# Ten bfloat16 products of the identity ahead of each step's product, in the sum stage and the two maximum stages of a four-layer graph network

## The chip, the cores and the metric

The kernel runs on one core of one Trainium2 chip. The metric is the device time of one launch in microseconds (us), lower is better. Two runs of the kernel before gave 13,217.70 and 13,255.61 us, median 13,236.66 us.

## The reference, cut to what matters

Four graph layers over 6,250 nodes with 96 features and 206,250 directed edges sorted by destination, each followed by a residual and a layer norm. The change touches the edge work of the second layer (a segment sum) and of the two convolutions in the third (segment maxima):

```
# layer 1: sum over the edges of each node
msg  = relu(x[src] + edge_attr @ We + be)
aggr = segment_sum(msg, dst, num_segments=n)
h    = relu((x + aggr) @ W1 + b1) @ W2 + b2      # then batch norm, relu
...
# layer 2: twice, maximum over the edges of each node
msg  = x[src] @ W_msg + edge_attr @ W_edge
agg  = segment_max(msg, dst, num_segments=n)
c    = leaky_relu(where(isneginf(agg), 0, agg) + x @ W_root + b)
```

All of it is float32. Layer 0 is an attention over edges with a segment softmax, layer 3 a graph attention layer; neither is touched.

## The kernel before, in words

The program is a row of stages, each ended by a barrier: preparation, the edge stage of layer 0 (lines 685 and on, matmuls of lines 805, 812 and 829), a node stage, then `edge_pass("e1")` (sum), a node stage, `edge_pass("e2a")` (maximum), a node stage, `edge_pass("e2b")` (maximum), a node stage, the edge stage of layer 3 (line 1741 and on, matmuls of lines 1854, 1864 and 1868), and the last node stage.

`edge_pass` (line 1079) handles 1,024 edges in a step `s`, 202 steps a stage. Each engine runs its own queue in order and meets the others at semaphores:

- **POOL** issues eight indirect DMAs a step (line 1151), 128 rows of 96 floats each, from `x_tab` into `got[s % 3]`. Before the eight of step `s` it waits until the add of step `s - 3` is done (`v_add`).
- **SP** loads the edge attributes four steps ahead (line 1117, `load_attr(s + 4)`), the masks every second step (line 1122), and stores the results of step `s - 2` (line 1126), in this order. `load_attr(s + 4)` waits on `t_attr` at `s + 1`, the signal that the product of step `s` is finished.
- **PE** (TensorE) waits for the attributes of step `s` and for `v_add` at `s - 1`, so for the add of step `s - 2`, which read the same buffer `EA[s % 2]`. Every fourth step up to 49 times it first writes one node tile (a transpose at line 1166, or the product with the root weights at line 1164) into the free columns of `EA[s % 2]`. Then two float32 products of 128 x 128 by 128 x 384 (line 1168) go into the two banks of `EA[s % 2]`; the second adds one to `t_attr`. A float32 product stands in the trace as two MATMUL records, so a step has four, and a product with the root weights adds two.
- **DVE** (VectorE) waits in `add(s)` on `t_attr` at `s + 1` and on the landing of the eight gathers, empties the node tile where there is one (lines 1181, 1183, 1185), and adds `EA` and `got` (line 1187, `v_add`). It then transposes (line 1193), scans three times (line 1202) and transposes back (line 1210). In the sum stage ACT (ScalarE) applies the relu between add and transpose (line 1227).

In every stage of this kind two engines wait on the same value of `t_attr`: SP for `load_attr(s + 4)` and DVE for `add(s)`. A wait that the trace cannot match to a signal's source is shown as "remote".

Of the kernel before, what the change touches and what calls it, by code (L numbers as in the profile page):

```python
# [24 lines left out]
BF16 = mybir.dt.bfloat16  # L25
# [6 lines left out]
P = 128  # L32
# [69 lines left out]
def build(nc, t, n_nodes, n_edges, D, DE):  # L102
# [54 lines left out]
    with ExitStack() as top:  # L157
# [10 lines left out]
        def keepb(name, shape, dt=F32):  # L168
            return top.enter_context(nc.sbuf_tensor(name, shape, dt))

        X = keepb("X", [P, NT, D])
        R = keepb("R", [P, NT, D])
        ident = keepb("ident", [P, P])
        ones_f = keepb("ones_f", [1, P])
        eps_col = keepb("eps_col", [P, 1])
        part_col = keepb("part_col", [P, 1])
# [508 lines left out]
        with Phase("e0", group="edge") as ph, Phase("find0", group="node") as pf:  # L685
# [64 lines left out]
            def after(e, sem, count):  # L750
                if count > 0:
                    e.wait_ge(sem, count)
# [326 lines left out]
        def edge_pass(name, relu, mask_row, op0, op1, edge_w, root=None):  # L1079

            with Phase(name, group="edge") as ph:
# [9 lines left out]
                EA = [ph.ps(f"EA{i}", [P, 2, CH]) for i in range(2)]  # L1091
# [17 lines left out]
                def root_tile(s):  # L1109
                    return s // EVERY if s % EVERY == 0 and s // EVERY < NT else None  # L1110

                with nc.Block() as block:
                    @block.sync
                    def _(e):
                        def load_attr(s):
                            after(e, t_attr, s - RA + 1)
                            e.dma_start(attr[s % RA][:, :], t["attr_S"][s]).then_inc(s_attr[s % RA], 16)

                        def load_mask(b):
                            after(e, v_scan, 2 * (b - RM + 1))  # L1120
                            for i in range(4):
                                e.dma_start(mask[b % RM][32 * i:32 * i + 32, :], mask_c[i, b:b + 1].to_broadcast([32, MB * CHS])).then_inc(s_mask[b % RM], 16)

                        def store(s):
                            e.wait_ge(v_back, s + 1)
                            e.dma_start(out_c[s], out[s % 3][:, :, :].rearrange("p k d -> p (k d)")).then_inc(s_st[s % 3], 16)

                        load_attr(0)
                        load_mask(0)
                        for s in range(1, RA):  # L1130
                            load_attr(s)
                        load_mask(1)
                        for s in range(NS):
                            if s + RA < NS:
                                load_attr(s + RA)
                            if s % 2 == 0 and s // 2 + 2 < NB:
                                load_mask(s // 2 + 2)
                            if s >= 2:
                                store(s - 2)
                        store(NS - 2)  # L1140
                        store(NS - 1)
                        for i in range(3):
                            e.wait_ge(s_st[i], 16 * len(range(i, NS, 3)))
# [11 lines left out]
                    @block.tensor  # L1155
                    def _(e):
                        for s in range(NS):
                            e.wait_ge(s_attr[s % RA], 16 * (s // RA + 1))
                            after(e, v_add, s - 1)
                            q = root_tile(s)  # L1160
                            if q is not None:
                                after(e, root_done, q)
                                if root:
                                    e.matmul(EA[s % 2][:, 0, K * D:K * D + D], xT_all[:, q * P:(q + 1) * P], root_w[:, :], start=True, stop=True).then_inc(t_root, 1)
                                else:
                                    e.transpose(EA[s % 2][0:D, 0, K * D:K * D + P], X[:, q, :], ident[:, :]).then_inc(t_root, 1)
                            for h in range(2):
                                ins = e.matmul(EA[s % 2][:, h, 0:K * D], attr[s % RA][:, h * P:(h + 1) * P], edge_w[:, :], start=True, stop=True)  # L1168
                            ins.then_inc(t_attr, 1)
# [1060 lines left out]
```

## Time and profile before

| | |
|---|---|
| median of two runs | 13,236.66 us |
| span of the profiled execution | 13,179.5 us |
| busy PE, DVE, ACT, POOL | 4,527.1, 6,535.8, 1,994.5, 8,151.7 us |
| share of the span | 34%, 50%, 15%, 62% |
| mean granted TensorE clock | 0.541 of full speed |
| mean DMA throughput | 96 GB/s |

The span runs from the first to the last instruction of one profiled execution; the device time holds 57.2 us more than it. Busy time is what an engine spent inside instructions. The starts of PE's records are measured, their ends are modelled. "Idle before" is the gap ahead of an instruction on its engine, and the name behind the arrow is what ended it.

### The profile page before, as it was taken

What the parts mean: (1) busy time and instruction counts of PE and PEld (TensorE: products, weight loads), DVE (VectorE), ACT (ScalarE), POOL (GpSimd) and SP (SyncE); (2) the same over time, 40 slices, a digit from 0 to 9 for tenths busy, and PEclk for the clock granted to TensorE, in tenths of its full rate; (3) what the DMA queues carried; (4) which work ended last, traced back from release to release, by engine and by line L of the source; (5) the groups of instructions that cost most, each with busy time, mean ns of one, the idle gap of its engine ahead of it and who ended that gap; (6) DMA issues with size and microseconds to landing.
All of it is one profiled execution on the core that took longest, in us unless ns stands there. A gap on an engine that the chain in (4) does not pass through costs nothing. (4 is left out here: it accounts for less than half of the span.)

```text
span 13179.5 us, 81573 instructions
## 1 busy us (share of the span) xinstructions
PE 4527.1 (34%) x15877; PEld 3022.1 (23%) x15877; DVE 6535.8 (50%) x10237; ACT 1994.5 (15%) x4360; POOL 8151.7 (62%) x8551
## 2 busy tenths in 40 slices
PE   3354455555222222232222222222222234434443
PEld 3244344444110111111111111111111123333332
DVE  9543344444544454454445455444544544444445
ACT  3233333333100000010000000000000022222223
POOL 1455555555676666656666666766666666666665
PEclk7555555555555555555555555555555555555555
DMA  2355555555333333323333332333333222222222
GB/s 76 106 155 154 149 152 155 153 159 152 99 86 82 87 89 87 88 72 85 87 87 93 81 91 79 87 85 88 89 87 86 81 58 66 69 68 68 68 69 63
DMA packets 1007936, 1264.02 MB, mean 96 GB/s; under 512 B 483123, under 2 KB 740467, under 8 KB 1007331
## 3 DMA queue, kind: packets, MB, share of 16 engines
q0 software_dynamic: 303696, 520.91, 17.5%
q1 hardware_dynamic: 638139, 635.93, 14.8%
q10 hardware_dynamic: 65600, 101.96, 2.7%
q8 instruction: 136, 2.23, 0.1%
q14 instruction: 365, 2.99, 0.1%
HBM read 829.46 MB, written 428.44 MB: 95 GB/s over the span
## 5 line engine op out<-in xcount | busy, mean ns | idle before, releaser
L789 POOL DMA_INDIRECT e_got<-kv_tab,dst_cols x1661 | 1574.5, 948 | 1281.7 <-DVE e_pay L894 770.2
L1843 POOL DMA_INDIRECT e_got<-h_tab,src_tcols x1612 | 1540.9, 956 | 881.8 <-issue 473.8
L1151 POOL DMA_INDIRECT e2a_got<-x_tab,src_cols x1616 | 1531.3, 948 | 775.7 <-issue 556.2
L1151 POOL DMA_INDIRECT e_got<-x_tab,src_cols x1616 | 1553.5, 961 | 718.3 <-issue 586.9
L1151 POOL DMA_INDIRECT e2b_got<-x_tab,src_cols x1616 | 1531.3, 948 | 745.7 <-issue 518.8
L1168 PE MATMUL e2b_EA<-we_W_edge,e2b_attr 128*128 128x384 f32 x808 | 574.9, 866 | 1331.2 <-DVE e2b_emsg L1187 728.3
L1168 PE MATMUL e_EA<-we_We,e_attr 128*128 128x384 f32 x808 | 578.3, 871 | 1297.8 <-issue 898.1
L1168 PE MATMUL e2a_EA<-we_W_edge,e2a_attr 128*128 128x384 f32 x808 | 572.0, 862 | 1300.4 <-issue 767.3
L894 DVE TENSOR_TENSOR e_pay<-e_got,e_Q 128x384 f32<-128x384 f32 x416 | 230.2, 553 | 1570.4 <-ACT e_Q L962 1129.1
L1940 DVE TENSOR_TENSOR_SCAN e_run<-e_Z,e_run,e_msg 98x512 f32<-98x512 f32 x404 | 516.9, 1279 | 795.4 <-ACT e_msg L2005 619.8
L805 PE MATMUL e_Q<-e_window,e_pick 128*128 128x96 f32 x3328 | 758.9, 408 | 79.1 <-issue 41.2
L805 PEld LDWEIGHTS e_Q<-e_window,e_pick 128*128 128x128 f32 x3328 | 744.0, 327 | 84.8 <-issue 82.8
L812 PE MATMUL e_B<-ident,e_run 100*128 100x100 f32 x1664 | 374.5, 379 | 904.4 <-issue 493.3
L1854 PE MATMUL e_B<-ident,e_run 98*128 98x98 f32 x1616 | 357.1, 374 | 759.2 <-DVE e_run L1940 627.7
L1168 PEld LDWEIGHTS e2b_EA<-we_W_edge,e2b_attr 128*128 128x128 f32 x808 | 236.8, 323 | 1621.6 <-issue 1620.1
L829 PE MATMUL e_M<-ident,e_pay 128*100 128x128 f32 x1664 | 445.8, 422 | 470.0 <-DVE e_pay L894 366.4
L1168 PEld LDWEIGHTS e_EA<-we_We,e_attr 128*128 128x128 f32 x808 | 239.7, 327 | 1590.5 <-issue 1590.2
L1168 PEld LDWEIGHTS e2a_EA<-we_W_edge,e2a_attr 128*128 128x128 f32 x808 | 235.8, 321 | 1589.1 <-issue 1587.1
L845 DVE TENSOR_TENSOR_SCAN e_run<-e_keep,e_run,e_M 100x512 f32<-100x512 bf16 x416 | 532.3, 1280 | 11.5 <-issue 7.2
L1187 DVE TENSOR_TENSOR e2a_emsg<-e2a_EA,e2a_got 128x768 f32<-128x768 f32 x202 | 191.9, 950 | 692.4 <-remote 458.4
L1187 DVE TENSOR_TENSOR e2b_emsg<-e2b_EA,e2b_got 128x768 f32<-128x768 f32 x202 | 192.1, 951 | 671.5 <-remote 396.5
L1187 DVE TENSOR_TENSOR e_emsg<-e_EA,e_got 128x768 f32<-128x768 f32 x202 | 192.7, 954 | 648.3 <-remote 529.4
(373 smaller groups left out, 10316.0 us busy)
## 6 DMA issues: line engine op xcount, KB each, us to landing
scan_out<-e_out SPq DMA_DIRECT2D x416, 200.0 KB
e_window<-q_tab SPq DMA_DIRECT2D x1664, 48.0 KB
scan_out<-e_out SPq DMA_DIRECT2D x404, 196.0 KB
scan_out<-e_out SPq DMA_DIRECT2D x202, 384.0 KB
scan_out<-e2a_out SPq DMA_DIRECT2D x202, 384.0 KB
scan_out<-e2b_out SPq DMA_DIRECT2D x202, 384.0 KB
e_rel<-rel_row ACTq DMA_DIRECT2D x208, 256.0 KB
e_keep<-keep_row ACTq DMA_DIRECT2D x208, 200.0 KB
```

Source lines behind the costliest of these rows:

```text
L789: e.indirect_dma_start(got[i][:, k, :], None, kv_tab, bass.IndirectOffsetOnAxis(dst_c[:, c * K + k:c * K + k + 1], axis=0)).then_inc(s_g[i ...
L805: ins = e.matmul(Q[c % 3][:, k * D:(k + 1) * D], pick[c % 4][:, k, :], window[c % U][:, k, :], start=True, stop=True)
L812: ins = e.transpose(B[c % 2][:, k * PAY:(k + 1) * PAY], run[c % 3][:, k::K], ident[0:PAY, 0:PAY])
L829: ins = e.transpose(M[c % 3][0:PAY, k * P:(k + 1) * P], pay[c % 4][:, k, :], ident[:, :])
L845: e.tensor_tensor_scan(run[c % 3][:, :], keep[c // 2 % KR][:, at:at + CH], M[c % 3][0:PAY, :], run[(c + 2) % 3][:, CH - 1:CH], ALU.mult, A ...
L894: e.tensor_tensor(pay[c % 4][:, :, 0:D].rearrange("p k (h d) -> p k h d", h=HEADS), got[c % RG0][:, :, D:2 * D].rearrange("p k (h d) -> p ...
L1151: e.indirect_dma_start(got[s % RS][:, k, :], None, x_tab, bass.IndirectOffsetOnAxis(src_cols[:, q:q + 1], axis=0)).then_inc(edge_got[s % R ...
L1168: ins = e.matmul(EA[s % 2][:, h, 0:K * D], attr[s % RA][:, h * P:(h + 1) * P], edge_w[:, :], start=True, stop=True)
L1187: e.tensor_tensor(emsg[s % 3][:, :, :].rearrange("p (h k) d -> p h (k d)", h=2), EA[s % 2][:, :, 0:K * D], got[s % RS][:, :, :].rearrange( ...
L1843: e.indirect_dma_start(got[c % RG][:, k, :], None, h_tab, bass.IndirectOffsetOnAxis(src_tcols[:, q:q + 1], axis=0)).then_inc(s_g[c % RG], 16)
L1854: ins = e.transpose(B[v % 2][:, k * HW:(k + 1) * HW], run[v % 2][:, k::K], ident[0:HW, 0:HW])
L1940: V[v].give(e.tensor_tensor_scan(run[p][:, :], Z[p][0:HW, :], msg[p][:, :], run[q][:, CH - 1:CH], ALU.mult, ALU.add), "scan")
```

## The change

A helper `keep_busy` issues `n` matmuls whose weights and moving data are both views of the float32 identity read as bfloat16: 128 x 128 weights, 128 x 512 moving (two rounds over the 256 bfloat16 words of a row). In `edge_pass`, PE calls it with `n = 10` on the second bank of `EA[s % 2]`, behind the two waits of the step and ahead of the node tile and the product. The step's second product overwrites the bank's first 384 columns, and nothing reads the others there. The ten signal nothing. Each has its own weight load, so a step has 20 instructions of PE more.

```
+        ident_words = ident[:, :].bitcast(BF16)
+        def keep_busy(e, bank, n):
+            for i in range(n):
+                e.matmul(bank, ident_words[:, 0:P], ident_words.unsqueeze(1).to_broadcast([P, 2, 2 * P]), start=True, stop=True)
...
                         for s in range(NS):
                             e.wait_ge(s_attr[s % RA], 16 * (s // RA + 1))
                             after(e, v_add, s - 1)
+                            keep_busy(e, EA[s % 2][:, 1, :], 10)
                             q = root_tile(s)
```

## Rows read from the trace of the kernel before

**Rows 1.** The page, its first line.
```profile
span 13179.5 us, 81573 instructions
```

**Rows 2.** The view of line 1187 (the add): duration ns min/median/max, first and last start us.
```profile
L1187 DVE TENSOR_TENSOR e_emsg<-e_EA,e_got x202: 915/957/959, 3452.0 to 5711.5; 128x768 f32<-128x768 f32 x101
L1187 DVE TENSOR_TENSOR e2a_emsg<-e2a_EA,e2a_got x202: 910/956/959, 5854.8 to 8107.1; 128x768 f32<-128x768 f32 x101
L1187 DVE TENSOR_TENSOR e2b_emsg<-e2b_EA,e2b_got x202: 911/957/959, 8218.6 to 10476.5; 128x768 f32<-128x768 f32 x101
...
  remote: 1384.2, 284
```

**Rows 3.** Windows, gathers of line 1151 alone: POOL busy (count), PEclk, DMA share, GB/s.
```profile
3440.00:3640.00 200.00, 151.09 (x160) 0.54 0.35 96
...
5843.00:6003.00 160.00, 120.94 (x128) 0.55 0.35 95
6060.00:6260.00 200.00, 131.06 (x135) 0.53 0.30 80
```

**Rows 4.** Timeline, early in stage e2a: start us, us, engine, line, xcount [idle before].
```profile
5877.43 2.82 PE L1168 MATMUL e2a_EA<-we_W_edge,e2a_attr 128*128 128x384 f32 x4
...
5880.28 0.33 SPq L1117 DMA_DIRECT2D e2a_attr<-in_attr_S  x1
...
5884.55 0.96 DVE L1187 TENSOR_TENSOR e2a_emsg<-e2a_EA,e2a_got 128x768 f32<-128x768 f32 x1 [3.05 <-DMA e2a_got<-x_tab,src_cols]
```

**Rows 5.** Timeline, 300 us later in the same stage.
```profile
6154.10 0.35 SPq L1117 DMA_DIRECT2D e2a_attr<-in_attr_S  x1
6154.11 0.96 DVE L1187 TENSOR_TENSOR e2a_emsg<-e2a_EA,e2a_got 128x768 f32<-128x768 f32 x1 [5.59 <-remote]
...
6155.21 2.90 PE L1168 MATMUL e2a_EA<-we_W_edge,e2a_attr 128*128 128x384 f32 x4 [7.93 <-issue]
...
6164.07 0.94 POOL L1151 DMA_INDIRECT e2a_got<-x_tab,src_cols  x1 [0.30 <-issue]
6169.49 0.33 SPq L1117 DMA_DIRECT2D e2a_attr<-in_attr_S  x1
6169.50 0.32 DVE L1185 SCALAR_TENSOR_TENSOR R<-e2a_EA,rstd_all,r_l2b 128x96 f32<-128x96 f32 x1 [9.76 <-remote]
...
6170.83 2.90 PE L1168 MATMUL e2a_EA<-we_W_edge,e2a_attr 128*128 128x384 f32 x4 [12.72 <-DVE e2a_emsg L1187]
```

**Rows 6.** Timeline of SP, the next three loads of attributes.
```profile
6182.09 0.35 SPq L1117 DMA_DIRECT2D e2a_attr<-in_attr_S  x1
...
6193.29 0.33 SPq L1117 DMA_DIRECT2D e2a_attr<-in_attr_S  x1
...
6204.52 0.35 SPq L1117 DMA_DIRECT2D e2a_attr<-in_attr_S  x1
```

**Rows 7.** Windows: PE, PEld, DVE, ACT, POOL busy (count), PEclk, DMA share, GB/s.
```profile
6165.10:6169.40 4.30, 0.00 (x0) 0.00 (x0) 0.00 (x0) 0.00 (x0) 0.00 (x0) 0.50 0.05 11
5740.00:5840.00 100.00, 58.52 (x192) 38.35 (x192) 66.62 (x263) 42.87 (x79) 35.05 (x35) 0.74 0.16 39
...
2100.00:2900.00 800.00, 428.32 (x1926) 371.12 (x1925) 365.04 (x601) 252.05 (x600) 455.89 (x482) 0.52 0.56 156
11000.00:13000.00 2000.00, 825.38 (x4524) 640.69 (x4522) 950.83 (x2417) 521.12 (x1090) 1272.60 (x1338) 0.54 0.27 68
```

**Rows 8.** Timeline, a catching-up stretch of stage e2a, two adds in turn.
```profile
6373.40 0.91 DVE L1187 TENSOR_TENSOR e2a_emsg<-e2a_EA,e2a_got 128x768 f32<-128x768 f32 x1
...
6378.91 0.92 DVE L1187 TENSOR_TENSOR e2a_emsg<-e2a_EA,e2a_got 128x768 f32<-128x768 f32 x1
```

**Rows 9.** Groups of PE by form of line 1864: busy us, mean ns of one.
```profile
L1864 PE MATMUL e_Z<-e_parts,e_sel 80*98 80x128 bf16 x1616 | 252.2, 308 | 113.3 <-issue 74.0 <-DVE e_mid L1979 25.4 <-DVE e_parts L1981 10.5
```

**Rows 10.** Timeline, layer 3's edge stage.
```profile
12013.95 0.70 PE L1854 MATMUL e_B<-ident,e_run 98*128 98x98 f32 x4
...
12017.33 0.50 ACT L1999 ACTIVATE e_out<-e_B 128x392 f32<-128x392 f32 x1 [4.85 <-remote]
...
12061.43 0.63 PE L1864 MATMUL e_Z<-e_parts,e_sel 80*98 80x128 bf16 x4
```

## The prediction

> **What bounds the kernel now.** I read the view of the add first, since each of the three stages repeats one add per step. From first to last add a stage takes 2259.5, 2252.3 and 2257.9 us [rows 2], over 201 intervals: 11.24, 11.21 and 11.23 us a step. Then the gathers, the one engine with enough work to fill that: a gather takes 0.94 us and 0.30 us of gap [rows 5], so eight need at least 9.92 us. The windows say that POOL reaches its pace only at the start of a stage. It issues 160 gathers in the first 200 us of the sum stage and 128 in the first 160 us of e2a, 10.0 us a step both times. From 6060 to 6260 us it issues 135 in 200 us, 11.9 us a step [rows 3]. Something other than POOL costs 1.2 us a step on average.
>
> Two timelines name it. Early in e2a the product starts at 5877.43 and its records end at 5880.25. SP, which waits on `t_attr`, goes at 5880.28, and DVE's next add is released by a landing gather [rows 4]. So the product's signal comes on time there, and nobody on the path wants it. 300 us later SP and DVE start within 0.01 us of each other, at 6154.10 and 6154.11 and again at 6169.49 and 6169.50; DVE's waits are "remote" now [rows 5]. The one semaphore that `load_attr(s + 4)` and `add(s)` share is `t_attr`, at the same value. Just before the second of these pairs nothing runs: from 6165.10 to 6169.40 all five engines are at 0.00, and the DMA share is 0.05 [rows 7]. The last gather was issued at 6164.07 and POOL cannot go on, as its next gather waits for this add. So the add waits for the product's signal.
>
> The records of PE hide this. The only product recorded between the two adds, 6155.21 to 6158.11 [rows 5], is not even the one awaited at 6169.5: that one, by the double buffer, was issued after the add before 6154.11. **The signal comes some 20 us after the product's recorded start.** Four steps with one node tile take from 6154.10 to 6204.52 [rows 5, 6], 50.4 us for 16 records of products and two of the tile: 2.8 us a record, where on time four take 2.82 us together [rows 4]. Steps of 11.20 us between signals (6182.09 to 6193.29, [rows 6]) are four such records. TensorE's signals leave at a quarter of the rate at which it seems to work. DVE's waits of this kind sum to 1384.2 us in 284 cases [rows 2]; that is no saving yet, because DVE would wait for gathers instead.
>
> **When does it lag?** Not behind dense matmul work. A stretch of a node stage has 192 records in 100 us with a clock of 0.74 [rows 7], and the stages that follow start on time. In a late stretch a step has 4.5 records in 12.6 us. The edge stages of layers 0 and 3 give 1926 records in 800 us and 4524 in 2000 us, 0.42 and 0.44 us a record [rows 7]. They lag at times (line 1854 ends at 12014.65, its reader goes at 12017.33 on "remote", 2.7 us late [rows 10]), but cannot be at 2.8 us a record. I take it that sparse work on TensorE brings the lag, which is argued from these densities and not shown. The granted clock does not tell it: it is 0.53 to 0.55, mostly the 1.2 GHz level, in early and late windows alike [rows 3].
>
> The Trainium skill ("TensorE: Matmul & The Clock Gate", section "Seeing it yourself") warns that the recorded clock events are unreliable and that the clock has been seen stuck at K=1/4; by that a product of 2.82 us would take 11.3, and the trace agrees in size, with 11.20.
>
> **The change, part by part.** It adds ten matmuls a step, 606 steps, and removes nothing.
> *Their time on PE.* The nearest bfloat16 rows: four of 128 columns take 0.63 us [rows 10], one takes 0.308 [rows 9], so they start (0.63 - 0.31)/3 = 0.107 us apart, and 512 columns take 0.43. Ten are 4.3 us. Bound from above: four float32 records of 384 columns take 2.82 us [rows 4], 0.70 each, scaled to 512 columns 0.94, ten 9.4. Bound from below: half of 4.3, at the 2.4 GHz level. I take 4.3, the same type. A step of PE is then 4.3 + 2.9 = 7.2 us, with a node tile of two records (another 0.7) 7.9, under the 10.0 of POOL.
> *On the path?* The product starts behind the add of step `s - 2` and is needed by the add of step `s`, 20 us later. 20 less 7.9 leaves 12 us of cover, also for the 2.7 us of lag in rows 10. If the cover goes, a step costs what PE takes.
> *First step of a stage.* PE needs 4.3 + 0.7 + 2.9 = 7.9 us; eight gathers need 9.92 and a landing. Hidden.
> *SP.* `load_attr(s + 4)` waits 4.3 us longer, and the masks and the store of step `s - 2` stand behind it. The store was ready when DVE ended its chain of 5.5 us [rows 8]; it now goes up to 3 us later. Its buffer is needed three steps on, 30 us; the attributes are needed four steps on. Nothing.
> *DVE, ACT, POOL.* No instruction more; the ten write a bank whose reader is done. Nothing, while a step of DVE (5.5 us [rows 8]) stays under 10.0.
> *The gain.* If 7.2 us of work in 10 keeps TensorE out of the lag, the gathers pace every step as in the first 160 to 200 us: 201 x 10.0 = 2010 us a stage. Saved: 249.5 + 242.3 + 247.9 = 739.7 us. The span goes from 13,179.5 [rows 1] to 12,439.8; the device time holds 57.2 us more (the median, 13,236.7, less the span), so **12,497 us**, 5.6% less. Late next are the gathers. At 9.92 us a step it would be 48 us less; at 10.3, with relapses, 180 us more.
>
> **The rivals.** What about 2% separates from no change, some 265 us.
> *1. Half a cure (0.15).* The lag returns in a part of the steps, as in layer 3's edge stage, which has a record each 0.44 us and still lags. Against it: 12 us of cover. At half the gain, 12,870 us.
> *2. No effect (0.13).* The lag has a cause outside TensorE's load. For it: the last edge stage lags with a dense load. Against it: on-time starts of the stages. The ten fill idle time: 13,237 us.
> A page's rule gives the same. By the Trainium skill, same page, Part 1, activity lifts the clock from 1.2 to 2.4 GHz. That would halve a recorded product of 2.9 us which the records show hidden in 11.2, and so change nothing; the trace speaks against reading the records so, since the add does wait for the signal [rows 5].
> *3. Slower (0.17).* The lag stays and charges the ten as it charges the others. The place is the same wait of the add. A step has 14.5 records instead of 4.5, and gets slower than 11.22 us if a record takes over 0.77 us on average. At 2.8 us it adds 28 us to each late step, with 9 in 10 of 606 late 15,300 us: 28,500 us in all. Against it: 0.42 us a record in the dense stages. A milder form needs no lag: at the float32 rate a step of PE is 9.4 + 2.9 + 0.2 = 12.5 us, 603 x 1.28 = 770 us more, 14,010 us.
>
> **How the numbers follow.** The cure has 0.55, and a range of its own of 12,420 to 12,700 (9.92 and 10.3 us a step, with the spread of the runs). Faster by over 2%: 0.55 and 0.15, together 0.70. Within 2%: 0.13. Slower: 0.17. The range from 12,420 to 13,280 takes in the cure, the half and no effect, and leaves out the slower cases.
>
> **What would show it.** Right: 8 gathers in 10.0 us through all three stages; DVE's waits before line 1187 end by gathers, not "remote"; SP and DVE no longer start together; stage lengths near 2010 us. The granted clock may rise to the 2.4 GHz level, which is no part of the sum. Wrong: equal starts of SP and DVE stay, with steps of 11.2 us (rival 2) or near 40 (rival 3); or PE's records of the ten lie more than 0.8 us apart.

## The result, and the profile after

The change made the kernel slower by 1.3%: median 13,408.4 us (13,400.8 to 13,416.0) against 13,236.7 us, ratio 1.0131, 95% interval 1.0099 to 1.0163. That is clear of the spread of these runs, two of each kernel, and less than 2%. I had forecast 12,497 us and a range up to 13,280.

The kernel before took 13,110 to 13,240 us in three sessions of this study (a session is a row of kernels run on one chip) and 11,236 us in three others, so the times of whole runs are compared with the kernel before of the same session, and I call the two kinds **late** and **on time**, after what the signals of TensorE do there. The pair of the forecast is from a late session; beside the kernel before at its best, 11,236 us, the change is worth nothing either way (eight runs, ratio 0.9999, below).

The page of the changed kernel, its first line, and then the view of the add, line 1194 in this kernel (columns as in [rows 2]):

```profile
span 13414.1 us, 93693 instructions
```

```profile
L1194 DVE TENSOR_TENSOR e_emsg<-e_EA,e_got x202: 902/920/958, 3444.5 to 5763.8; 128x768 f32<-128x768 f32 x101
L1194 DVE TENSOR_TENSOR e2a_emsg<-e2a_EA,e2a_got x202: 903/926/959, 5910.9 to 8228.7; 128x768 f32<-128x768 f32 x101
L1194 DVE TENSOR_TENSOR e2b_emsg<-e2b_EA,e2b_got x202: 903/945/959, 8345.2 to 10661.8; 128x768 f32<-128x768 f32 x101
its engine sat idle before it (us, times) until:
  remote: 2502.6, 153
  issue: 14.1, 2
  DMA e2a_got<-x_tab,src_cols: 4.0, 1
```

The stages last 2319.3, 2317.8 and 2316.6 us, 59.7, 65.5 and 58.7 more than in [rows 2]: 184.0 us together (from the starts before rounding), 11.53 us a step for 11.23. The span grew by 234.6 us, the median time by 171.7. Of the span's other 50.6 us, 49.3 lie behind the last add, where the code is the same; that part scatters from run to run (section on the experiments), so I don't put it down to the change.

The waits for the product did not go, they grew: "remote" 2502.6 us in 153 cases, for 1384.2 in 284. A timeline of the changed kernel, 320 us into e2a, shows the new form of what [rows 5, 6] show:

```profile
6203.80 0.35 SPq L1123 DMA_DIRECT2D e2a_attr<-in_attr_S  x1
6203.81 0.96 DVE L1194 TENSOR_TENSOR e2a_emsg<-e2a_EA,e2a_got 128x768 f32<-128x768 f32 x1 [1.40 <-remote]
...
6225.45 0.94 POOL L1157 DMA_INDIRECT e2a_got<-x_tab,src_cols  x1 [0.30 <-issue]
6231.83 0.33 SPq L1123 DMA_DIRECT2D e2a_attr<-in_attr_S  x1
6231.84 0.96 DVE L1194 TENSOR_TENSOR e2a_emsg<-e2a_EA,e2a_got 128x768 f32<-128x768 f32 x1 [22.39 <-remote]
...
6232.94 4.25 PE L179 MATMUL e2a_EA<-ident 128*128 128x512 bf16 x10 [22.73 <-DVE e2a_emsg L1194]
6233.06 0.94 POOL L1157 DMA_INDIRECT e2a_got<-x_tab,src_cols  x1 [6.67 <-DVE e2a_emsg L1194]
...
6237.41 0.91 DVE L1194 TENSOR_TENSOR e2a_emsg<-e2a_EA,e2a_got 128x768 f32<-128x768 f32 x1
...
6243.11 0.95 DVE L1194 TENSOR_TENSOR e2a_emsg<-e2a_EA,e2a_got 128x768 f32<-128x768 f32 x1
...
6248.66 0.91 DVE L1194 TENSOR_TENSOR e2a_emsg<-e2a_EA,e2a_got 128x768 f32<-128x768 f32 x1
```

SP and DVE still start within 0.01 us of each other. One signal is 28.0 us after the last; then three adds follow 5.6 us apart, which is DVE catching up at its own chain [rows 8]. POOL ran 24 gathers ahead, until its three buffers were full, and stood 6.67 us. Only TensorE's signal is late here: the add ends at 6232.80, and the two engines that wait for it go on at 6232.94 (TensorE) and 6233.06 (POOL). The ten took 4.25 us in this step, as costed, and 3.0 us on average in e2a (608.4 us in 202 steps). And the good start of a stage is gone (windows of the gathers alone, columns as in [rows 3]):

```profile
3440.00:3640.00 200.00, 132.25 (x141) 0.72 0.28 79
5900.00:6100.00 200.00, 134.53 (x144) 0.70 0.28 79
```

141 and 144 gathers in 200 us where [rows 3] have 160: the steps that used to run at 10.0 us run at 11.1 and 11.3. The clock rose meanwhile, from 0.54 to 0.70 in these windows (by the whole program, 0.541 to 0.628), so for much of the time to the 2.4 GHz level, and bought nothing. The Trainium skill ("TensorE: Matmul & The Clock Gate", Part 1) says that activity lifts the clock; the trace agrees, and by that rule alone the time stays as it was, which is nearer than what I forecast.

### The profile page after: what moved, and what is told of

It is laid out like the page before. It is cut to its first block and busy times, and to the rows that moved or that the text cites. A ratio compares the mean times of both kernels' runs of the same rounds, so it can differ in the third digit from the quotient of the medians.

```text
span 13414.1 us, 93693 instructions
## 1 busy us (share of the span) xinstructions
PE 5524.0 (41%) x21937; PEld 3489.0 (26%) x21937; DVE 6497.5 (48%) x10237; ACT 1997.8 (15%) x4360; POOL 8106.7 (60%) x8551
## 5 line engine op out<-in xcount | busy, mean ns | idle before, releaser
L1157 POOL DMA_INDIRECT e_got<-x_tab,src_cols x1616 | 1526.4, 945 | 809.9 <-issue 482.9
L179 PE MATMUL e_EA<-ident 128*128 128x512 bf16 x2020 | 646.2, 483 | 1473.8 <-DVE e_emsg L1194 1060.7
L179 PE MATMUL e2a_EA<-ident 128*128 128x512 bf16 x2020 | 608.4, 461 | 1439.7 <-DVE e2a_emsg L1194 1230.1
L179 PE MATMUL e2b_EA<-ident 128*128 128x512 bf16 x2020 | 614.5, 465 | 1419.1 <-DVE e2b_emsg L1194 1222.6
L179 PEld LDWEIGHTS e_EA<-ident 128*128 128x128 bf16 x2020 | 221.3, 116 | 1898.5 <-issue 1708.3
L179 PEld LDWEIGHTS e2a_EA<-ident 128*128 128x128 bf16 x2020 | 215.2, 112 | 1835.5 <-issue 1703.2
L179 PEld LDWEIGHTS e2b_EA<-ident 128*128 128x128 bf16 x2020 | 216.5, 113 | 1819.9 <-issue 1693.2
L818 PEld LDWEIGHTS e_B<-ident,e_run 100*128 100x128 f32 x1664 | 269.4, 221 | 894.9 <-issue 872.1
```

Source lines behind the costliest of these rows:

```text
L179: e.matmul(bank, ident_words[:, 0:P], ident_words.unsqueeze(1).to_broadcast([P, 2, 2 * P]), start=True, stop=True)
L818: ins = e.transpose(B[c % 2][:, k * PAY:(k + 1) * PAY], run[c % 3][:, k::K], ident[0:PAY, 0:PAY])
L1157: e.indirect_dma_start(got[s % RS][:, k, :], None, x_tab, bass.IndirectOffsetOnAxis(src_cols[:, q:q + 1], axis=0)).then_inc(edge_got[s % R ...
```

## The experiments

My theory, as forecast: sparse work on TensorE brings the late signal, and enough work cures it. Rivals: the lateness has nothing to do with TensorE's load; or each record of TensorE is charged; or the double buffer `EA` is what makes a late signal cost.

### Second late session (before: 13,113.5 us)

In the second and the third late session no trace of the kernel before was kept, so the stages are set against [rows 2], 2256.6 us on average, from the first. Three late kernels of the two in which TensorE has as many instructions as before (three buffers, no loads, thin product, all below) have 2257.5, 2255.7 and 2258.7 us, so this base holds within some 2 us. Whole times scatter more, also where the code is the same.

The product read in bfloat16, half as many records of TensorE:

```
-    ins = e.matmul(EA[s % 2][:, h, 0:K * D], attr[s % RA][:, h * P:(h + 1) * P], edge_w[:, :], ...)
+    ins = e.matmul(EA[s % 2][:, h, 0:K * D], attr[s % RA][:, :].bitcast(BF16)[:, 2 * h * P + 1:2 * (h + 1) * P:2],
+                   edge_w[:, :].bitcast(BF16)[:, 1::2], ...)
```

> The kernel before, with one edit: the step's product reads the upper halves of attributes and weights as bfloat16, so the messages are rounded inputs' products. Theory A (in a late stretch TensorE finishes its work at a fixed slow rate, 2.8 us a float32 record, and the add waits for that): the product has two bfloat16 records in place of four float32 ones, about a quarter of the work, 3 us; the signal leaves the path, steps take 10.0 us by the gathers, 12,500 us in all. Theory B (the signal comes a fixed 20 to 25 us after the issue, and two buffers make 11.2 us a step of that): no change, 13,237 us.

13,091.0 us. Its view of the add (without its other rows), and windows of its gathers:

```profile
L1188 DVE TENSOR_TENSOR e2a_emsg<-e2a_EA,e2a_got x202: 946/958/959, 5774.7 to 8001.5; 128x768 f32<-128x768 f32 x101
...
its engine sat idle before it (us, times) until:
  DMA e2b_got<-x_tab,src_cols: 804.8, 152
  DMA e2a_got<-x_tab,src_cols: 792.0, 150
```

```profile
5760.00:5960.00 200.00, 148.93 (x158) 0.50 0.35 100
6100.00:6300.00 200.00, 150.39 (x143) 0.50 0.31 88
7000.00:7200.00 200.00, 149.94 (x144) 0.50 0.31 88
```

This is the cure that I wanted from the ten products, with no "remote" wait left in 606 adds, and it is worth 30 us a stage (2226.7 for 2256.6), not 247; the whole run is 22.5 us shorter than its own before. After some 200 us the adds wait for gathers instead, at 11.1 to 11.2 us a step. The windows say how: POOL is as busy as at the start (150 us of 200), but with 143 gathers in place of 158, 1.04 to 1.05 us each instead of 0.94. So with the late signal off the path a pace of nearly 11.2 us is left, and it is the gathers'. I saw them slow in this kernel only: the mean issue in e2a is 1.040 us here, 0.948 in the kernel before and 0.944 in the changed kernel.

A third buffer for `EA`, paid with the second one of `F`:

```
-    EA = [ph.ps(f"EA{i}", [P, 2, CH]) for i in range(2)]
-    F = [ph.ps(f"F{i}", [P, 2 * CH]) for i in range(2)]
+    EA = [ph.ps(f"EA{i}", [P, 2, CH]) for i in range(3)]
+    F = [ph.ps("F0", [P, 2 * CH])] * 2
...
-    after(e, v_add, s - 1)
+    after(e, v_add, s - 2)
```

> The kernel before with three EA buffers (the two F buffers become one), so that a product is issued three adds ahead. Theory A (slow rate of work): the rate stays 11.2 us a product, no change, 13,237 us. Theory B (fixed delay of 20 to 25 us): the delay is spread over three steps, under 10.0 us each, so the gathers pace and the time is 12,500 us.

13,175.0 us, stages of 2259.2, 2255.5 and 2257.8: no change in the stages, though the whole run is 61.5 us longer than its own before. An earlier product does not help. That fits a pace of the signals and not a fixed delay that a buffer can hide.

My two kernels on TensorE's load. Two products a step in place of ten (`keep_busy(..., 2)`):

> The changed kernel with two products of the identity in place of ten. Theory A: two more records of 512 bfloat16 columns are charged about 1.7 us each in a late stretch (as ten and a product take 28.8 us there in the changed kernel): steps of about 16 us when late; if late stretches stay as long as before, 15,300 us; if the load shortens them as ten does, between 13,237 and 14,500 us. Theory B: 13,237 us.

13,191.6 us, stages of 2268.3, 2269.7 and 2266.8: 11.7 us more than [rows 2] on average, and 78.1 us more than its own before in all. Theory A had named 15,300 us, or at the least more than 13,237.

Fourteen products, two behind each of the first seven gathers of a step, meant to leave TensorE no long idle stretch:

```
-    keep_busy(e, EA[s % 2][:, 1, :], 10)
+    for j in range(1, 8 if s + 1 < NS else 0):
+        e.wait_ge(tick, 8 * (s + 1) + j)      # POOL adds one behind each gather
+        keep_busy(e, EA[s % 2][:, 1, :], 2)
```

> The changed kernel with fourteen products of the identity a step, two behind each of the first seven gathers that POOL issues for the step after (a count that POOL raises behind each gather), in place of ten in one block. If an even load keeps the signal on time (theory C): about 10.1 us a step, 12,550 us, DVE's waits end by gathers. If the load doesn't heal and theory A charges 1.7 us a record: 35 us in late steps, above 20,000 us. If only the mean load counts: like the changed kernel, 13,400 us.

13,439.2 us, stages of 2350.1, 2351.8 and 2346.2, 92.8 us more than before, the worst of all. The edit did not do what I meant. POOL runs up to three steps ahead, so most of the counts that TensorE waits for were reached already, and the fourteen mostly came in one block (in e2a they start within 6 us of each other in 167 of 200 cases); where they were not reached, their wait holds the product back as well. A timeline of e2a:

```profile
7024.01 1.48 PE L1179 MATMUL e2a_EA<-we_W_edge,e2a_attr 128*128 128x384 f32 x4
...
7040.89 0.96 DVE L1198 TENSOR_TENSOR e2a_emsg<-e2a_EA,e2a_got 128x768 f32<-128x768 f32 x1 [16.18 <-remote]
...
7042.05 5.76 PE L179 MATMUL e2a_EA<-ident 128*128 128x512 bf16 x14 [16.56 <-POOLq L1160]
```

TensorE stands idle for 16.56 us here, and so an even load was never tried. What the run does show is that much more work is no cure: in a window of 200 us TensorE is busy for 103.2 us, where the kernel before has 54.9 (its window is in the third late session), and the late signals stay (PE, PEld, DVE, ACT, POOL busy (count), clock, DMA share, GB/s):

```profile
7000.00:7200.00 200.00, 103.20 (x309) 38.78 (x309) 94.31 (x108) 0.00 (x0) 126.42 (x134) 0.72 0.29 84
```

### First on-time session (before: 11,235.7 us)

Ten products of 64 columns, as many instructions in an eighth of the columns; twenty wide products; before without its steady loads; before with a thin product:

```
-    e.matmul(bank, ident_words[:, 0:P], ident_words.unsqueeze(1).to_broadcast([P, 2, 2 * P]), ...)
+    e.matmul(bank[:, 0:64], ident_words[:, 0:P], ident_words[:, 0:64], ...)
```

> The changed kernel with ten products of 64 columns in place of 512: the same instructions, an eighth of the columns. By stage, first to last add (before 2257, changed 2318 us): if the number of TensorE's instructions sets the extra, 2318 us stays; if their columns do, about 2265 us, and the steady step is 11.2 us as before.

```
-    keep_busy(e, EA[s % 2][:, 1, :], 10)
+    keep_busy(e, EA[s % 2][:, 1, :], 20)
```

> The changed kernel with twenty products a step. If the extra grows with the work (two products gave 11 us a stage, ten 61): about 2380 us a stage and 13,600 us in all. If TensorE kept busier gets out of the late stretches: below the changed kernel, down to 2020 us a stage.

```
-    if s + RA < NS:
-        load_attr(s + RA)
-    if s % 2 == 0 and s // 2 + 2 < NB:
-        load_mask(s // 2 + 2)
+    if s == 0:
+        load_mask(2)
```

> The kernel before with the loads of attributes and masks left out after the first ones of a stage (old data is used again; the waits on them go too). Theory D (a step's pace of 11.20 us in the long run is set by something that all transfers of the step share, and TensorE's late signal only shows it): the pace goes to 10.0 us, 2010 us a stage, some 12,450 us. If TensorE's own late signal sets the pace, or the gathers alone do: 11.2 us stays.

```
+    n = K * D if s < 2 else 16
-    ins = e.matmul(EA[s % 2][:, h, 0:K * D], attr[s % RA][:, h * P:(h + 1) * P], edge_w[:, :], ...)
+    ins = e.matmul(EA[s % 2][:, h, 0:n], attr[s % RA][:, h * P:(h + 1) * P], edge_w[:, 0:n], ...)
```

> The kernel before with the product cut to 16 of its 384 columns after the first two steps (the rest of the messages is stale): as many TensorE records as before, hardly any columns. Theory D: as with the bfloat16 product the signal is on time and the steps are still 11.2 us, 2227 us a stage. If the records' number makes the signal late: 2257 us a stage with remote waits.

11,234.3, 11,242.8, 11,233.8 and 11,243.2 us, with stages of 2006.9 to 2008.9 in all four. None of the edits is seen, and neither is any late signal; a step takes 9.99 us on average. The last two work on stale data, so their results are others than the reference's. These four could not tell the theories apart, but they showed that the 11.2 us a step is not the program's.

### Second on-time session (before: 11,236.6 us, nine runs)

The changed kernel itself, once more:

> The changed kernel itself, unaltered, once more beside the kernel before on one chip. Two levels of the kernel before have been seen: about 13,110 to 13,240 us with steps of 11.20 us in the long run (where the signals of TensorE come late), and 11,235.7 us with steps of 9.99 us (where they come on time). Theory: the ten products cost only where the signals come late. Where the kernel before is at 11.2 us a step: three stages of about 2,318 us, the program 150 to 210 us above before on the same chip. Where it is at 9.99 us a step: TensorE's 7.2 to 7.9 us a step stay under the gathers, the stages stay within 3 us of 2,007 us each and the program within 20 us of before. Rival, the ten products cost about 60 us a stage wherever they run, by their 20 instructions a step: about 2,070 us a stage, 184 us more, on either chip.

Eight runs, 11,235.5 us, ratio 0.9999, interval 0.9988 to 1.0010. The view of the add, and a timeline of e2a:

```profile
L1194 DVE TENSOR_TENSOR e2a_emsg<-e2a_EA,e2a_got x202: 946/958/959, 4838.2 to 6845.0; 128x768 f32<-128x768 f32 x101
...
its engine sat idle before it (us, times) until:
  DMA e2b_got<-x_tab,src_cols: 594.3, 153
  DMA e2a_got<-x_tab,src_cols: 592.7, 153
```

```profile
5103.43 1.48 PE L1175 MATMUL e2a_EA<-we_W_edge,e2a_attr 128*128 128x384 f32 x4
...
5104.94 0.33 SPq L1123 DMA_DIRECT2D e2a_attr<-in_attr_S  x1
...
5107.26 0.96 DVE L1194 TENSOR_TENSOR e2a_emsg<-e2a_EA,e2a_got 128x768 f32<-128x768 f32 x1 [3.27 <-DMA e2a_got<-x_tab,src_cols]
5108.36 3.25 PE L179 MATMUL e2a_EA<-ident 128*128 128x512 bf16 x10 [3.45 <-DVE e2a_emsg L1194]
```

This is the picture that I had forecast for the changed kernel: SP goes 0.03 us after the product's end (5104.91), DVE waits for gathers, and a stage takes 2007 us (I had said 2010). But the kernel before takes as long here. The ten cost nothing under the gathers' pace.

Beside it ran the narrow ten (11,236.4 us), the twenty (11,238.1) and the kernel without loads (11,234.6), all with stages of 2006.8 to 2007.3:

> The ten products with 64 moving columns and 64 weight columns in place of 512 and 128: as many instructions, an eighth of the columns, about 0.5 us of TensorE a step in place of 4.3. Where the signals come late: if the price goes by the time that TensorE is held (4.3 us ahead of the product), the stages fall back to 2,255 to 2,265 us, as in the kernel before; if it goes by instructions (20 more a step in both), they stay at about 2,318 us. Where they come on time: 2,007 us a stage by either.

> Twenty wide products a step in place of ten: some 8.6 us of TensorE at the half clock ahead of a product of 2.9 us, together 11.5 us, more than a gathers' step of 9.99 us if the clock stays at half, or 4.3 + 1.5 us if it is granted in full. Where the signals come late: by the price of ten (61 us a stage over the kernel before) twice, about 2,380 us a stage; if the fuller engine at last brings the signals on time, 2,010 to 2,050 us. Where they come on time: 2,007 us a stage.

> The kernel before without its steady loads of attributes (512 KB a step) and masks: all steps after the first few work on the first tiles' data, so the maxima and sums are others. It tells whether the long run's 11.20 us a step is a budget that the gathers share with the plain loads. Where the signals come late: if they share it, the steps shorten towards 10.0 us (about 2,010 to 2,100 us a stage); if the gathers alone or TensorE's signals set it, 11.20 us a step stay (2,250 us a stage). Where they come on time: 2,007 us a stage, by either.

### Third late session (before: 13,223.4 us)

> Ten products of 64 moving columns and 64 weight columns: as many instructions as in the changed kernel, about 0.5 us of TensorE a step in place of 4.3. Where before is at 13,100 us or more: if the price of the ten goes by the time that TensorE is held, 2,255 to 2,265 us a stage, as before; if by the 20 instructions a step, about 2,318 us. Where before is at 11,236 us: 2,007 us a stage, as twice already.

13,364.9 us. (The edit narrows only the moving columns; the weights keep their 128 x 128, as the row below shows, where the expectation speaks of 64 weight columns.) The narrow ten, first the group of its products in e2a (busy us, mean ns), then its adds:

```profile
L179 PE MATMUL e2a_EA<-ident 128*128 128x64 bf16 x2020 | 128.5, 227 | 1686.6 <-DVE e2a_emsg L1194 1124.2
```

```profile
L1194 DVE TENSOR_TENSOR e_emsg<-e_EA,e_got x202: 908/916/959, 3417.3 to 5734.1; 128x768 f32<-128x768 f32 x101
L1194 DVE TENSOR_TENSOR e2a_emsg<-e2a_EA,e2a_got x202: 909/946/959, 5878.8 to 8197.7; 128x768 f32<-128x768 f32 x101
...
  remote: 2183.2, 155
```

The wide ten keep TensorE busy for 608.4 us in that stage:

```profile
L179 PE MATMUL e2a_EA<-ident 128*128 128x512 bf16 x2020 | 608.4, 461 | 1439.7 <-DVE e2a_emsg L1194 1230.1
```

With 128.5 us in place of 608.4 the stages are as long: 2316.7, 2318.9 and 2316.9, for 2319.3, 2317.8 and 2316.6. The wide ten in the third late session too, beside a bfloat16 product, have 2320.6 us on average (below). **At the same number of instructions the price is the same, whatever columns TensorE works through**, and it does not go by its clock (0.549 here, 0.628 there). Each product is a matmul and a weight load; no run parts the two.

> The kernel before without its steady loads of attributes and masks (all steps after the first few use the first tiles' data). Where before is at 13,100 us or more: if 11.20 us a step are a budget that gathers share with plain loads, 2,010 to 2,100 us a stage; if the gathers or TensorE's signals set it by themselves, 2,226 to 2,255 us. Where before is at 11,236 us: 2,007 us.

13,232.4 us, stages of 2259.9, 2258.8 and 2248.3. In the window from 7000 to 7200 us the traffic is 71 GB/s, for 94 in the kernel before; the steps are the same. The plain loads have no part that can be seen in the 11.2 us. The window of the kernel before, then that of the kernel without loads (PE, PEld, DVE, ACT, POOL busy (count), clock, DMA share, GB/s):

```profile
7000.00:7200.00 200.00, 54.86 (x87) 23.87 (x88) 107.96 (x122) 0.00 (x0) 135.93 (x145) 0.56 0.34 94
```

```profile
7000.00:7200.00 200.00, 53.00 (x80) 22.34 (x80) 100.20 (x113) 0.00 (x0) 133.34 (x141) 0.54 0.24 71
```

> The kernel before with a product of 16 columns in place of 384 after the first two steps (the other columns keep what the first steps wrote, so the output is another). Where before is at 13,100 us or more: if the size of TensorE's work makes the signals late, they come on time and the stage goes to the 2,226 us of the run with a bfloat16 product; if it is a floor of the gathers and signals, 2,226 to 2,255 us as well but with the waits for TensorE kept. Less than 2,200 us would show that TensorE's work slows the gathers. Where before is at 11,236 us: 2,008 us.

13,223.9 us, stages of 2261.8, 2253.6 and 2260.8, with a product of 16 columns. As many instructions, as long, and the late signals stay ("remote" 1578.0 us in 313 cases).

> The changed kernel, ten products kept, with the edge product read in bfloat16 (2 records a step in place of 4; the output differs in the last digits). Where before is at 13,100 us or more: if the ten cost only by making a late signal of the product later still, the stage stays at 2,227 us, as the bfloat16 product alone gave, since the add then waits for gathers; if they also slow the gathers or their landing, 2,260 to 2,320 us. Where before is at 11,236 us: 2,007 us.

13,407.9 us, stages of 2321.5, 2323.7 and 2316.6, with 2157.2 us of "remote" waits in 160 cases. Next to the bfloat16 product alone (2226.7, no such wait, second late session) the ten bring the late signals back and cost 94 us a stage. So they are not only charged where a product was late already.

The last 50 us of the first section: behind the last add the kernel without loads has 2749.9 us and the one with the thin product 2747.8, the changed kernel 2752.3, the kernel before 2703.0, the one with two products 2698.3, all with the same code there. That part scatters by this much.

### Third on-time session (before: 11,235.8 us)

Meant for a late one: whether any engine's instructions are charged, and whether the charge is in proportion.

```
+    after(e, a_spare, s)
+    for i in range(20):
+        ins = e.activation(spare[:, 8 * i:8 * i + 8], ident[:, 8 * (i % 16):8 * (i % 16) + 8], ACT.Relu)
+    ins.then_inc(a_spare, 1)
```

> The kernel before, TensorE untouched, with twenty small operations of ScalarE (128 x 8, results that nothing reads) behind each step's add in the three stages; in the sum stage behind the relu. Nobody waits for them, save the next step's on ScalarE. Where before is at 13,100 us or more: if any engine's instructions are paid for as TensorE's are (15 ns each, 20 a step), about 2,316 us a stage and 180 us more in all; if only TensorE's are, 2,250 to 2,262 us a stage, as before. Where before is at 11,236 us: 2,007 us a stage.

> Twenty wide products a step, 40 instructions of TensorE. Where before is at 13,100 us or more: if the price is in proportion to instructions (61 us a stage for 20), 2,256 + 122 = about 2,378 us a stage; if it has levelled off, 2,318 to 2,330 us; if TensorE's own 11.5 us a step at the half clock bound it, 2,330 to 2,400 us with waits of one step each. Where before is at 11,236 us: 2,008 us, as seen.

11,235.1 and 11,235.7 us; all stages 2006.9 to 2007.4. Both questions stay open. Twenty products are 40 instructions of TensorE a step, and are hidden where the signals are on time.

## Why the prediction was wrong

*The reading of before held in the main.* In the long run the add waits for the product's signal, and the signal comes some 20 us late; gathers at 9.99 us a step are what is left when it doesn't (2007 us a stage in three sessions, against my 2010). The costs of the edit held: ten products 4.25 us in the step shown for 4.3 forecast, nothing on SP, DVE or POOL of its own.

Two sums were off, and neither decided the matter. The 57.2 us that I added for device time over span compare two different executions: where both stand on record for one execution, the time is 1.9 us over the span (13,415.96 for 13,414.1), so the traced execution of the kernel before took about 13,181 us (an estimate from that). And the 2.82 us of the product stand at the 1.2 GHz level already (1.48 us in the on-time timeline, with the clock up). K=1/4, of which the Trainium skill warns in the section that I cited, would be half of that level and make them 5.6 us, not 11.3, so the agreement with 11.20 that I noted is none.

*The step that failed* is "I take it that sparse work on TensorE brings the lag, which is argued from these densities and not shown." I had compared stages that differ in everything, and made density the cause. Four things speak against it now. Three to four times the records cure nothing (259 and 309 in the window of 200 us with ten and fourteen products, 87 before), and each kernel is slower. A product of 16 columns is no worse than before (2258.7 us on average for 2256.6). In three sessions the same sparse work has no lag at all. And the dense edge stage of layer 0, where nothing was changed, is slowed in the late sessions too: 4532 records of TensorE in 2000 us, for 6195 on time. These are the kernel before, late, and then the changed kernel, on time (columns as in [rows 7]):

```profile
500.00:2500.00 2000.00, 999.90 (x4532) 866.66 (x4532) 857.92 (x1414) 656.89 (x1612) 1115.08 (x1177) 0.52 0.55 152
```

```profile
500.00:2500.00 2000.00, 1232.31 (x6195) 1130.51 (x6195) 1167.00 (x1941) 881.76 (x2145) 1512.40 (x1601) 0.62 0.75 207
```

So the lag that I wanted to cure in three stages is a state of the whole execution. The kernel before loses 763 us ahead of the first add and 421 behind the last one against an on-time run with the same code there (act_twenty), and some 748 in the three stages. The on-time first 160 to 200 us of a stage, my main evidence, were no result of the dense node stage ahead of them either: with twenty more instructions a step they went away, behind the same node stage.

*The second step that failed* is that a signal on time is worth 247 us a stage. In a late session it was worth 30, since behind it the gathers ran at nearly 11.2 us a step as well. I read POOL's floor off 160 us at the start of a stage and carried it through 2250.

*The rivals.* Half a cure (0.15) had nothing to it: the waits for the signal grew. No effect (0.13) had its mechanism right: "the lag has a cause outside TensorE's load". Slower (0.17) had the direction and the place, the same wait of the add, and a price far too high: I took 2.8 us a record from the late signals themselves. The measured price is small, and in the stages it goes with the number of instructions, each product being a matmul and a weight load:

| kernel | instructions more, a step | a stage, mean us | more than [rows 2] | ns each | whole run, more than before of its session |
|---|---|---|---|---|---|
| two | 4 | 2268.3 | 11.7 | 14.6 | 78.1 |
| ten, wide | 20 | 2317.9 | 61.3 | 15.2 | 171.7 |
| ten, narrow | 20 | 2317.5 | 60.9 | 15.1 | 141.6 |
| fourteen | 28 | 2349.4 | 92.8 | 16.5 | 325.7 |

"ns each" is the difference over 201 steps and the instructions of one; the base is the mean of [rows 2], 2256.6. Wide against narrow is the firm pair. The proportion is argued: the whole runs don't follow it (one run each, save the wide ten), the kernel with fourteen has eight semaphore instructions of POOL and seven waits of TensorE a step besides, and a product held back, and the bfloat16 product has 4 instructions fewer and gains 29.9 us, 37 ns each. With this price the sum would have been 13,237 + 606 x 0.30 = 13,419 us; 13,408 were measured.

*What stays open* is the cause of the late signals and slow gathers in some sessions. The Trainium skill ("NOTIFIC — the notification-queue block", section 7.1) describes a path that would fit: engines report events to memory, and where that path backs up it holds the engine. For it: the price by count and not by length, the good first 200 us, as if something had to fill first, and its loss with more instructions. Against a plain limit on all records: no loads, no gain; and the edge stage of layer 0, though slowed, keeps going at 2.4 records of PE a microsecond in the same execution [rows 7], where e2a has 0.44 (87 in 200 us, the window above). No run here looked at that path, and I claim nothing for it. The runs list a span and a clock, so they were recorded, and whether the recording itself has a part is open too. One other candidate that counts instructions does not fit: the fetching of the program. In the changed kernel 133 adds of the three stages come 20 to 40 us after the one before, and in only 36 of these intervals does a transfer of the instruction queues begin; there is none in the wait up to 6231.84 above.

No kernel of this study clearly beats the kernel before. The bfloat16 product's 13,091.0 for 13,113.5 is one run each, and less exact.

## What to carry to other kernels

A wait that ends on a late signal shows where the lateness is felt and not what makes it. Before an edit is priced by curing it, take the late part away by itself (here the bfloat16 product, one line) and see which floor is below. Filler work isn't free because its engine is idle: its price didn't depend on its columns here, so measure it with a narrow copy of the same count. Look in the trace whether an edit did what it was meant to do, as the fourteen products did not; and a gain or loss of one per cent may belong to a session, as the ratio was 1.0131 in one and 0.9999 in another.

## What the runs showed of the hardware

The same program took 11,236 us in three sessions and 13,110 to 13,240 in three others, 17 to 18% more, at nearly the same granted clock (the kernel without loads: 0.538 late, 0.571 and 0.584 on time). The third late and the third on-time session show the same number for their chip, so I can't say that it is a property of the chip. In the late sessions TensorE's signals come up to some 20 us after the recorded end, while VectorE's reach TensorE and POOL in 0.14 and 0.26 us (6232.80 to 6232.94 and 6233.06); in the on-time timeline above TensorE's signal comes within 0.03 us. With the bfloat16 product of the late session an indirect DMA's issue grows from 0.94 to 1.05 us; in the other late kernels its mean in e2a stays at 0.94 to 0.95. Twenty products a step lifted the clock most, and moved nothing (the last kernel of the third on-time session; PE, PEld, DVE, ACT, POOL, clock, DMA share, GB/s):

```profile
6000.00:6200.00 200.00, 138.84 (x497) 59.76 (x496) 111.90 (x125) 0.00 (x0) 151.24 (x161) 0.85 0.37 99
```
